# Small attentions of a two-layer kernel: keys masked once per group, scores contracted over 32 partitions

## The chip, the cores and the metric

The kernel runs on one core of a Trainium2 chip. The metric is the device time of one execution, in microseconds (us). Three runs of the kernel before gave a median of 2568.2 us (2562.18 to 2571.58). All data are float32 unless said otherwise.

## What is computed

The input x has 64 sequences of 64 rows with 128 features. Two layers run over it; the part that the change touches are two attentions with 16 heads of 8 features, in which every query row attends to 64 key rows:

```
# layer 0, feed-forward block: attention across the batch, for each of the 64 positions
q, k, v = split(LN(x) @ in_proj.T + in_proj_b)        # 16 heads of 8
a = softmax(q @ k.T / sqrt(8)) ; o = a @ v             # then out_proj, LN, mixture of experts
# layer 1: attention along the sequence, for each of the 64 sequences, causal
q, k, v = split(LN(x) @ w_qkv)                         # 16 heads of 8
a = softmax(mask(q @ k.T) / sqrt(128)) ; o = a @ v     # then out_proj
```

Around them stand a gated delta rule, two cross attentions with 16 heads of 32 features (layer 0), two mixtures of experts with routing, and a block with eight weighted projections (layer 1).

## The kernel before, in words

The 64 sequences are worked on in 16 groups (G) of four blocks of 64 rows, and four slots (s = 0 to 3) hold four groups at a time, with two PSUM banks each. The program of a group is written for each engine as a Python generator, and `in_order` interleaves the four slots' generators by a table of digits, `ORDER`, one table per phase and engine: each digit says which slot gives the next step. Each engine executes its queue in just that order, and semaphores tie the engines together. The phases are:

1. "one": delta rule and both cross attentions (`pe_delta`, `pe_mha` and so on).
2. "across": the attention across the batch (`pe_across`, which calls `pe_small` with y = "c", not causal).
3. "last": routing and experts of layer 0 (`pe_tiles`), then per group the causal attention (`pe_attn1`, which calls `pe_small` with y = "n", causal), the weighted projections (`pe_xattn1`, lines 1476 and 1482), and routing and experts of layer 1.

A small attention of one group has 16 heads, taken as four quads g = 0 to 3. Features lie on partitions: head h has partitions 8h to 8h + 7, so quad g has partitions 32g to 32g + 31. For each quad POOL builds masked keys (`pool_km`, line 994): km holds, for each block b and each of the quad's four heads j, the 64 keys with all partitions but head j's set to zero by a 0/1 mask (`m8`). PE then multiplies (`pe_scores`, lines 1001 and 1002): the block's 64 queries, all 128 partitions of them, are the stationary operand, and the 4 x 64 masked keys the moving one, so that one matmul gives four heads' scores of a block, written to the lower or the upper 64 partitions of PSUM as b is even or odd. In the causal attention a bfloat16 matmul with a constant of 128 partitions (`CB`, line 1001) first writes the causal mask, and the scores are added to it. Then follow the row maximum and the subtraction on DVE (1007, 1009), the exponential on ACT (1371), four transposes on PE (1013), a copy on ACT (1374) and the products with V on PE (1022), which also write to 64 partitions each. km has one buffer per slot: POOL makes the masked keys of quad g + 1 when the scores of quad g are done (signal `a_s`), and PE waits for `m_km` before each quad.

The cross attentions of phase "one" use the same `pool_km` and `pe_scores` with heads of 32 features and their own mask `m32`.

A matmul's record in the profile names rows and columns: 128*64 is a stationary operand of 128 partitions (the contraction) and 64 columns (the output partitions); below, such a pair is called the matmul's tile. A float32 matmul leaves two records, a bfloat16 one leaves one.

Of the kernel before, what the change touches and what calls it, by code (L numbers as in the profile page):

```python
# [18 lines left out]
W = 128 * NT  # L19
# [13 lines left out]
def columns(parts):  # L33
    at, out = 0, {}
    for name, n in parts:
# [7 lines left out]
    ("laterT", 64), ("causal", 64), ("m32", 4), ("parity", 2), ("m8", 16), ("m24", 4), ("tri", 64), ("half", 1), ("before", 128), ("ones", 128), ("iota", 128), ("part", 1), ("back", 8),  # L43
# [53 lines left out]
            "vz.c m_km.c.0 m_km.c.1 m_km.c.2 m_km.c.3",  # L97
# [45 lines left out]
            "rstd.n vz.n m_km.n.0 m_km.n.1 m_km.n.2 m_km.n.3 n_bias.n rstd.h rstd.g",  # L143
# [21 lines left out]
            "110332200001311330303222200102100001111000133010022122013302020112031020201012312110301000122131212120332023102120021020030301130323200222030310313001"  # L165
            "303110201201121031221320302133202102011213221123123021022132013212302021031300210212102230300300333013002301231330201301013221313120102312232110130332"
            "122000021211212210213001313202032321313331311232331112322311133000033122230313023220030032021131100330100103330122022130323020112313110201221120012213"
            "302331221323121023232021330131113302023023003022030300303032030012012010302011323330120211012001221231113122032021301123100132203321001201023032001201"
            "303123113230200220301330130102313132301201131010031223110100321222103211210022121213132031022233123233231211323233111230020201311022230331210322030302"
            "303200303001131103301010222021333021213132312112230130200011221123133321231230210232023210013013001132033023022303001203130130030113023102011210312321"  # L170
            "333021021120100212121122122131310230122021323102132102303303002302330320123200103031002303110323103230112210321322021321033112012200212113200013221302"
            "101021233002312133313112323312311223111300300222330031320322030012032003030303022022333011112021010231332121132131010212200012122313321233121232012303"
            "103232003203310010301113030022303030300032302002032323033120210221002113231311212033013203123310032112201003012032303112032103020133013001321302303102"
            "1213201130323230120102213030211232210213311231223123231121312322133131231232133132131323232123213131312313",
        "act":
            "110223300001311330033002332203002120102211210113311022130220132031020012000001132110203110211100220003222220300131130031212021331122333000022121132312"
            "210302201332001012102122003033000301332001213032011123210211312023033102211210002221110230012303200203310313113323211122300133113003131222301312122110"
            "323202133122012203332021332303031330020001333213231321102320211011132200222300033000323120012130313313220000112122313103210220311300022100030323101011"
# [30 lines left out]
        "dve":  # L209
            "20330112202303201320130123001220033221023311321103120310231002233020120332110131023102100231022032102311323101313201302132130213",  # L210
        "pool":
            "013202320230321103012203311010223032312103100231321102032023013102031221033110202213130103213213",
    },
    "last": {
        "pe":
# [285 lines left out]
def build(nc, x, ctx, ctxk, itok, cst, col, row, wa, ws, wf, wx, wl, x1, ys, out):  # L501
    es = ExitStack()
    with es:
# [80 lines left out]
        sig = Signals(nc)  # L584
# [1696 lines left out]
```

## Time and profile before

| | us |
|---|---|
| median of 3 runs | 2568.2 |
| profiled execution, whole | 2576.1 |
| profiled execution, span of the core | 2574.3 |
| PE busy in the span | 2194.3 (85%) |
| DVE busy | 1830.5 (71%) |
| POOL busy | 1469.8 (57%) |
| ACT busy | 1145.6 (45%) |
| masked keys on POOL (line 994), 256 instructions | 486.7 |
| scores on PE (line 1002), 2048 records | 291.7 |

Busy time is the union of an engine's instructions. Lines are those of the kernel before; PEld is the loading of stationary operands, which lies beside PE. Phase "one" ends at about 1345 us of the span, "across" at 1505 us, and the causal attention has its first mask matmul at 1812.0 us and its last at 2275.1 us.

### The profile page before, as it was taken

The numbers are of one execution on the slowest core, as the hardware profiler recorded it, in microseconds if no ns is written. First come the engines' busy times: TensorE is split into PE (matmuls) and PEld (weight loads), VectorE is DVE, ScalarE is ACT, GpSimd is POOL, SyncE is SP. The second block draws the span as 40 slices with busy tenths as digits, with TensorE's granted clock in tenths as the row PEclk, the third lists the DMA queues.
The fourth block names the chain that finished last, engine by engine and source line by source line (L and its number), as shares of the span: only waits on it lengthen the run. The fifth ranks groups of instructions, "written<-read, shape, count | busy, mean of one in ns | idle before, by whom it ended". The sixth has DMA issues, their size and how long they took to land.

```text
span 2574.3 us, 62932 instructions
## 1 busy us (share of the span) xinstructions
PE 2194.3 (85%) x24908; PEld 1758.7 (68%) x24908; DVE 1830.5 (71%) x4790; ACT 1145.6 (45%) x2561; POOL 1469.8 (57%) x1568
## 2 busy tenths in 40 slices
PE   5988989899898998889989963897798998996972
PEld 3866668666677666776667752887576776786972
DVE  6688777888778878688757788333788788875232
ACT  5234574356743466534545520453343343443541
POOL 3775447665567654676557864357746433413465
PEclk8999999899999999999999965898898998997996
DMA  3000000000000000000000002797000000006992
GB/s 128 4 5 1 1 1 4 4 2 1 2 4 4 2 1 2 3 5 2 1 34 2 2 18 98 240 361 219 22 20 11 18 16 3 14 19 218 346 331 81
DMA packets 85589, 144.99 MB, mean 56 GB/s; under 512 B 23664, under 2 KB 60016, under 8 KB 85040
## 3 DMA queue, kind: packets, MB, share of 16 engines
q1 hardware_dynamic: 76208, 122.33, 14.0%
q0 software_dynamic: 9088, 18.63, 2.7%
q8 instruction: 199, 3.26, 0.5%
q14 instruction: 94, 0.77, 0.1%
HBM read 124.40 MB, written 16.52 MB: 55 GB/s over the span
## 4 chain that ended last, share of the span: by engine, by line
PE 54%; DVE 25%; POOL 9%; issue 7%; DMA 3%; ACT 2%; SPq 0%; POOLq 0%; DVEq 0%; ACTq 0%
PE PS L1002 7%; PE PS L637 5%; PE PS L1022 5%; PE PS L1013 4%; PE PS L1482 3%; PE PS L1476 3%; PE PS L1946 3%; PE PS L1930 3%; POOL GOT L1633 3%; PE PS L627 2%; PE PS L989 2%; DVE z L618 2%; PE PS L1097 2%; PE PS L1086 1%; PE PS L1103 1%
## 5 line engine op out<-in xcount | busy, mean ns | idle before, releaser
L994 POOL TENSOR_TENSOR km<-qk,Cs 128x1024 f32<-128x1024 f32 x256 | 486.7, 1910 | 290.2 <-ACT qk L1141 149.3
L1002 PE MATMUL PS<-km,qk 128*64 128x256 f32 x2048 | 291.7, 395 | 0.2 <-POOL km L994 0.2
L1959 ACT ACTIVATE wh<-PS,we 128x128 f32<-128x128 f32 x624 | 175.5, 373 | 231.4 <-PE PS L1930 231.2
L1866 POOL DMA_INDIRECT wx<-x,INV x156 | 149.0, 955 | 159.4 <-PE PS L1937 83.9
L1007 DVE TENSOR_REDUCE mx<-PS 128x8 f32<-128x512 f32 x256 | 176.0, 688 | 81.3 <-PE PS L1002 79.3
L1022 PEld LDWEIGHTS PS<-V,PT 128*64 128x64 f32 x4096 | 155.4, 140 | 68.0 <-issue 32.4
L1946 PE MATMUL PS<-we,wh 128*128 128x128 f32 x1248 | 176.6, 287 | 21.1 <-DVE wxT L1976 19.1
L1022 PE MATMUL PS<-V,PT 128*64 128x66 f32 (+1 forms) x4096 | 179.6, 224 | 13.7 <-DVE PT L1179 9.1
L1009 DVE TENSOR_TENSOR P<-PS,mx 128x512 f32<-128x512 f32 x256 | 177.0, 691 | 8.8
L1946 PEld LDWEIGHTS PS<-we,wh 128*128 128x128 f32 x1248 | 160.9, 200 | 27.9 <-DVE wxT L1976 25.2
L1013 PE MATMUL PS<-Cs,P 128*128 128x128 f32 x1024 | 163.2, 286 | 16.1 <-ACT P L1371 8.4
L1930 PE MATMUL PS<-wxT,we 128*128 128x128 f32 x1248 | 171.8, 285 | 5.5 <-issue 3.0
L1002 PEld LDWEIGHTS PS<-km,qk 128*64 128x64 f32 x2048 | 147.4, 140 | 40.7 <-issue 15.8
L622 POOL TENSOR_TENSOR xrs<-xrs,Cs 128x2 f32<-128x2 f32 x112 | 82.0, 732 | 146.8 <-DVE xrs L614 144.3
L1497 ACT ACTIVATE eh<-PS 128x256 f32<-128x256 f32 x256 | 96.9, 383 | 154.3 <-PE PS L1476 151.0
L1930 PEld LDWEIGHTS PS<-wxT,we 128*128 128x128 f32 x1248 | 159.6, 201 | 7.9 <-issue 4.8
L1013 PEld LDWEIGHTS PS<-Cs,P 128*128 128x128 f32 x1024 | 116.6, 144 | 55.7 <-issue 21.9
L1633 POOL DMA_INDIRECT GOT<-ys,POS x128 | 123.6, 965 | 51.7 <-issue 49.7
L1476 PE MATMUL PS<-exF,WX 128*128 128x256 f32 x512 | 150.3, 399 | 3.1 <-DVE X L1526 2.9
L1482 PE MATMUL PS<-WX,eh 128*128 128x128 f32 x1024 | 138.1, 281 | 0.5 <-ACT eh L1497 0.5
L1482 PEld LDWEIGHTS PS<-WX,eh 128*128 128x128 f32 x1024 | 132.4, 196 | 8.0 <-issue 2.3
L1141 ACT ACTIVATE qk<-PS 128x512 f32<-128x512 f32 x128 | 76.4, 597 | 118.6 <-PE PS L1071 93.0
(337 smaller groups left out, 5344.0 us busy)
## 6 DMA issues: line engine op xcount, KB each, us to landing
we<-in_wf SPq DMA_DIRECT2D x78, 578.0 KB, 6.7
we<-in_wl SPq DMA_DIRECT2D x78, 578.0 KB, 6.6
ys<-wy SPq DMA_DIRECT2D x156, 64.0 KB, 6.2
x<-X SPq DMA_DIRECT2D x32, 128.0 KB, 2.0
R<-in_wa SPq DMA_DIRECT2D x1, 3072.0 KB, 15.5
wx<-x,INV POOLq DMA_INDIRECT x156, 5.6
X<-in_x SPq DMA_DIRECT2D x4, 512.0 KB, 15.3
WX<-in_wx SPq DMA_DIRECT2D x1, 2048.0 KB, 7.7
```

The costliest lines, as they stand in the source:

```text
L994: return e.tensor_tensor(A.km.rearrange("p (b j t) -> p b j t", b=NB, j=4), bc(v3(A.qk[:, W:2 * W], NB), 2, 4), bc(bc(masks, 1, NB), 3, 64 ...
L1002: i = e.matmul(o, A.qk[:, 64 * b:64 * b + 64], A.km[:, W * b:W * b + W], not causal, True)
L1007: e.tensor_reduce(A.mx, S3, AX, ALU.max).then_inc(*o.inc())
L1009: return e.tensor_tensor(v3(A.P, NA), S3, bc(A.mx, 2, 64), ALU.subtract)
L1013: i = e.transpose(dst[:, 128 * k:128 * k + 128], A.P[:, 128 * k:128 * k + 128], ID)
L1022: i = e.matmul(dst[64 * (b % 2):64 * (b % 2) + 64, c0:c0 + 2 * D + 2], A.PT[:, q0:q0 + 64], A.V[:, 8 * b + 2 * g + k, :, :].rearrange("p h ...
L1476: e.matmul(o, w1[:, x_, 128 * f:128 * f + 128], B.xF, True, True).then_inc(*sig.inc(G, "h_up", x_, f))
L1482: i = e.matmul(o[:, 128 * t:128 * t + 128], h[:, W * f + 128 * t:W * f + 128 * t + 128], w2[:, x_, f, :], f == 0, f == 1)
L1633: e.indirect_dma_start(out=GOT[G % 2][:, t, k, :], out_offset=None, in_=ys[h], in_offset=bass.IndirectOffsetOnAxis(ap=POS[h][:, j:j + 1], ...
L1930: i = e.matmul(ps(s, 1)[:, 128 * f:128 * f + 128], w[:, 128 * f:128 * f + 128], B.xT, True, True)
L1946: i = e.matmul(ps(s, 0)[:, 0:128], B.h[:, 128 * f:128 * f + 128], w[:, 644 + 128 * f:772 + 128 * f], f == 0, f == 3)
L1959: i = e.activation(B.h[:, 128 * f:128 * f + 128], ps(s, 1)[:, 128 * f:128 * f + 128], ACT.Relu, bias=w[:, 512 + f:513 + f])
```

## The change

POOL masks the keys once per group instead of once per quad. The new mask has four columns: column j keeps the partitions of the j-th head of every quad at once, so km holds the masked keys of all four quads, each quad's in its own 32 partitions. `pe_scores` gets a slice of partitions k; in the small attentions quad g contracts over partitions 32g to 32g + 31 of qk and km alone. The mask matmul with `CB` is left as it is, with 128 partitions. PE waits for `m_km` once per group; POOL issues one instruction per group in place of four, and no longer waits for `a_s`. The cross attentions call `pe_scores` with its default, all 128 partitions. All the tables of `ORDER` are new.

```diff
-        def pe_scores(e, A, dst, causal=False):
+        def pe_scores(e, A, dst, causal=False, k=slice(0, 128)):
             for b in range(NB):
                 r = slice(64 * (b % 2), 64 * (b % 2) + 64)
                 o = dst[r, W * (b // 2):W * (b // 2) + W]
                 if causal:
                     e.matmul(o, CB[:, r], bc(CB[:, 128:192], 1, 4), True, False)
-                i = e.matmul(o, A.qk[:, 64 * b:64 * b + 64], A.km[:, W * b:W * b + W], not causal, True)
+                i = e.matmul(o, A.qk[k, 64 * b:64 * b + 64], A.km[k, W * b:W * b + W], not causal, True)
             return i
...
             for g in range(4):
-                e.wait_ge(*sig.at(G, "m_km", y, g))
+                if g == 0:
+                    e.wait_ge(*sig.at(G, "m_km", y))
                 e.wait_ge(*(sig.at(G, "a_pt", y, g - 1) if g else sig.at(G, "n_v", y)))
                 if causal:
                     e.wait_ge(*cb.now())
-                pe_scores(e, A, ps(s, 1), causal).then_inc(*sig.inc(G, "a_s", y, g))
+                pe_scores(e, A, ps(s, 1), causal, slice(32 * g, 32 * g + 32)).then_inc(*sig.inc(G, "a_s", y, g))
...
-            for g in range(4):
-                e.wait_ge(*(sig.at(G, "a_s", y, g - 1) if g else sig.at(G, "m_qk", y)))
-                pool_km(e, A, c("m8", 4 * g, 4 * g + 4)).then_inc(*sig.inc(G, "m_km", y, g))
-                yield
+            e.wait_ge(*sig.at(G, "m_qk", y))
+            pool_km(e, A, c("m8")).then_inc(*sig.inc(G, "m_km", y))
+            yield
...
-    parts["m8"] = (r // 8) == np.arange(16)[None, :]
+    parts["m8"] = (r // 8) % 4 == np.arange(4)[None, :]
```

What the tables and the quads make of the queues is seen at three places. The first is POOL in phase "across", some way into it; km_296, km_311, km_326 and km_341 are the masked keys of slots 0 to 3, V the values' buffers. Before:

```order
L982 MEMSET V_309 128x576
L984 COPY V_309<-Cs 128x64
L994 TENSOR_TENSOR km_311<-qk_310,Cs 128x1024
L994 TENSOR_TENSOR km_296<-qk_295,Cs 128x1024
L994 TENSOR_TENSOR km_341<-qk_340,Cs 128x1024
L994 TENSOR_TENSOR km_296<-qk_295,Cs 128x1024
```

After:

```order
L982 MEMSET V_309 128x576
L984 COPY V_309<-Cs 128x64
L995 TENSOR_TENSOR km_311<-qk_310,Cs 128x1024
L982 MEMSET V_294 128x576
L984 COPY V_294<-Cs 128x64
L995 TENSOR_TENSOR km_296<-qk_295,Cs 128x1024
```

POOL now has one masking per group between the clearings of two V buffers, where it had four.

The second place is PE in phase "across" (1002 scores, 1013 transposes, 1022 products with V; in the changed kernel each line is one higher). Before:

```order
L1022 MATMUL PS<-V_339,PT_347 64x18 x8
L1002 MATMUL PS<-km_341,qk_340 64x256 x4
L1013 MATMUL PS<-Cs,P_298 128x128 x4
L1022 MATMUL PS<-V_324,PT_332 64x18 x8
L1013 MATMUL PS<-Cs,P_313 128x128 x4
L1022 MATMUL PS<-V_294,PT_302 64x18 x8
L1002 MATMUL PS<-km_296,qk_295 64x256 x4
L1022 MATMUL PS<-V_309,PT_317 64x18 x8
L1002 MATMUL PS<-km_311,qk_310 64x256 x4
```

After:

```order
L1023 MATMUL PS<-V_339,PT_347 64x18 x8
L1023 MATMUL PS<-V_294,PT_302 64x18 x8
L1014 MATMUL PS<-Cs,P_328 128x128 x4
L1003 MATMUL PS<-km_296,qk_295 64x256 x4
L1003 MATMUL PS<-km_341,qk_340 64x256 x4
L1023 MATMUL PS<-V_324,PT_332 64x18 x8
L1014 MATMUL PS<-Cs,P_313 128x128 x4
L1003 MATMUL PS<-km_326,qk_325 64x256 x4
```

The same kinds of work alternate in another order of slots. Over the whole phase a row of one tile is followed by a row of another 134 times before (128*64 and 128*128 alone), and 209 times after, with the scores as 32*64.

The third place is PE at one quad's scores in the causal attention. Before:

```order
L1022 MATMUL PS<-V_294,PT_302 64x18 x8
L1001 MATMUL PS<-CB 64x256
L1002 MATMUL PS<-km_296,qk_295 64x256
L1001 MATMUL PS<-CB 64x256
L1002 MATMUL PS<-km_296,qk_295 64x256
```

After:

```order
L1998 MATMUL PS<-Wsm,noF_338 128x128 x2
L1002 MATMUL PS<-CB 64x256
L1003 MATMUL PS<-km_296,qk_295 64x256
L1002 MATMUL PS<-CB 64x256
L1003 MATMUL PS<-km_296,qk_295 64x256
```

The alternation of mask and scores, four times per quad, is unmoved; but the mask keeps its 128 partitions while the scores have 32.

## Rows read from the trace of the kernel before

**Rows 1.** The page: busy time, share and instructions of each engine.

```profile
span 2574.3 us, 62932 instructions
...
PE 2194.3 (85%) x24908; PEld 1758.7 (68%) x24908; DVE 1830.5 (71%) x4790; ACT 1145.6 (45%) x2561; POOL 1469.8 (57%) x1568
```

**Rows 2.** Stretches of the span: length, busy time by engine, granted clock, DMA.

```profile
core 0: us, PE busy (x) PEld busy (x) DVE busy (x) ACT busy (x) POOL busy (x), PEclk, DMA share, GB/s
0.00:1345.00 1345.00, 1197.80 (x15744) 910.78 (x15744) 1056.13 (x2413) 673.16 (x1285) 801.19 (x910) 0.96 0.03 10
1345.00:1505.00 160.00, 156.40 (x2064) 115.28 (x2064) 116.79 (x279) 91.80 (x169) 126.03 (x90) 0.99 0.01 2
1505.00:1812.00 307.00, 212.62 (x1586) 198.26 (x1586) 165.35 (x617) 95.99 (x334) 181.51 (x217) 0.79 0.60 199
1812.00:2280.00 468.00, 418.70 (x3851) 335.71 (x3852) 382.41 (x1100) 180.69 (x419) 222.23 (x206) 0.93 0.05 13
```

**Rows 3.** Groups of instructions: busy us, mean ns; idle before them and its enders.

```profile
L994 POOL TENSOR_TENSOR km<-qk,Cs 128x1024 f32<-128x1024 f32 x256 | 486.7, 1910 | 290.2 <-ACT qk L1141 149.3 <-PE PS L1002 110.0 <-ACT qk L1364 26.7
L1001 PE MATMUL PS<-CB 128*64 128x256 bf16 x256 | 39.9, 290 | 7.7 <-POOL km L994 4.7 <-issue 2.8
```

**Rows 4.** The chain of waits by line, 1345 to 1505 us, then 1812 to 2280 us.

```profile
by line: PE PS L1002 35.0%; PE PS L1022 20.7%; PE PS L1013 20.3%; PE PS L1335 4.5%; PE PS L989 4.4%; PE PS L1336 3.2%; PE PS L627 3.2%; ACT PT L1374 1.9%; ACT P L1371 1.2%; DVE mx L1007 0.9%; DVE P L1009 0.9%; DVE est L607 0.9%; issue 0.9%;
...
by line: PE PS L1476 15.4%; PE PS L1482 14.7%; PE PS L1002 8.1%; PE PS L1022 5.7%; issue 5.1%; PE PS L1013 5.0%; POOL GOT L1633 4.9%; POOL km L994 3.2%; DVE epr L1510 2.7%; PE PS L627 2.7%; PE PS L1001 2.6%; DVE X L618 2.6%; DVE ez L618 2.1
```

**Rows 5.** Who waited for whom, 1812 to 2280 us: us in total, times, longest.

```profile
POOL km L994 <- PE PS L1002: 95.9, 35, 12.3
...
PE PS L1001 <- POOL km L994: 4.7, 3, 2.5
```

**Rows 6.** Timeline of PE at one causal quad: start us, us from first start to last end.

```profile
2061.09 0.31 PE L1001 MATMUL PS<-CB 128*64 128x256 bf16 x2
2061.22 0.60 PE L1002 MATMUL PS<-km,qk 128*64 128x256 f32 x4
2061.65 0.28 PE L1001 MATMUL PS<-CB 128*64 128x256 bf16 x2
2061.76 0.60 PE L1002 MATMUL PS<-km,qk 128*64 128x256 f32 x4
2062.30 0.48 PE L1476 MATMUL PS<-exF,WX 128*128 128x256 f32 x1
```

**Rows 7.** Timeline of PE in the first cross attention, all tiles 128*128 until line 1002.

```profile
179.78 0.60 PE L1070 MATMUL PS<-zx,R 128*128 128x256 f32 x2
180.21 0.59 PE L1071 MATMUL PS<-zy,R 128*128 128x256 f32 x2
180.74 0.65 PE L1002 MATMUL PS<-km,qk 128*64 128x256 f32 x4
```

**Rows 8.** Timeline of PE in the second cross attention, with a tile of 64 rows.

```profile
889.48 0.60 PE L1070 MATMUL PS<-zx,R 128*128 128x256 f32 x2
890.01 0.70 PE L1071 MATMUL PS<-zy,R 64*128 64x256 f32 x2
890.63 0.94 PE L1086 MATMUL PS<-R,oF 128*128 128x128 f32 x6
```

**Rows 9.** Timeline of PE in phase "across".

```profile
1403.40 0.66 PE L1013 MATMUL PS<-Cs,P 128*128 128x128 f32 x4
1403.98 0.67 PE L1022 MATMUL PS<-V,PT 128*64 128x18 f32 x16
1404.47 1.08 PE L1002 MATMUL PS<-km,qk 128*64 128x256 f32 x8
1405.36 0.30 PE L1022 MATMUL PS<-V,PT 128*64 128x18 f32 x5
```

**Rows 10.** Granted clock and the same columns, the first 60 us.

```profile
core 0: us, PE busy (x), PEclk, DMA share, GB/s
20.00:40.00 20.00, 10.21 (x25) 0.70 0.23 65
40.00:60.00 20.00, 14.45 (x125) 0.70 0.01 1
60.00:80.00 20.00, 19.49 (x450) 1.00 0.01 3
```

More of the change, by code:

```diff
@@ L42 @@
     ("ident", 128), ("sl", 128), ("unit", 64), ("le", 64), ("nm0", 64), ("nm1", 64), ("nm2", 64), ("nm3", 64), ("nm4", 64), ("nn", 64),
-    ("laterT", 64), ("causal", 64), ("m32", 4), ("parity", 2), ("m8", 16), ("m24", 4), ("tri", 64), ("half", 1), ("before", 128), ("ones", 128), ("iota", 128), ("part", 1), ("back", 8),
+    ("laterT", 64), ("causal", 64), ("m32", 4), ("parity", 2), ("m8", 4), ("m24", 4), ("tri", 64), ("half", 1), ("before", 128), ("ones", 128), ("iota", 128), ("part", 1), ("back", 8),
 ])
@@ L96 @@
         "pool":
-            "vz.c m_km.c.0 m_km.c.1 m_km.c.2 m_km.c.3",
+            "vz.c m_km.c",
     },
@@ L142 @@
         "pool":
-            "rstd.n vz.n m_km.n.0 m_km.n.1 m_km.n.2 m_km.n.3 n_bias.n rstd.h rstd.g",
+            "rstd.n vz.n m_km.n n_bias.n rstd.h rstd.g",
     },
@@ L168 @@
[L168 to L171, printed above, removed]
@@ new lines @@
+        "pool":
+            "013210122330110022033100020030011100011100112222220000221122011002302001311332022302133311111332122033221203133321233003133302000311230011131022103112"
+            "222013000320032303302113001213110311223022000002200112203330310033332210110100112133111003121020022220121113223230012333211113310233222103312221232331"
+            "230033333231021000313110120312103101332200001311133322200213010213123230011202231022333000002200223301011111330011222110033001123221222111022000022011"
+            "221113013333032122233102133022332212333320012133303303002111301230130130221331002002223333002100111233110021130230222211330003300221002200331033122111"
+            "102101113000312132202220212000110223331221110133110233322213013221233022123333002332333110300201131102301310322101332222333320000111213321323222023333"
+            "23",
@@ L252 @@
         "sp":
[L253 to L255 removed]
+            "576a1348db02c9dddddddddddd1133dddd22001504150246260437041537263726150415372604263175150437260426371504371265043715260437152604371526043715260437152630"
@@ L256 @@
+            "471526043715260347152604371564756745ab98dddda9b8ab9dddd8bdddda93382211dddd0037263726043715372615043701542615042637150426153702463175042615370426153704"
+            "2615042637153720641504263715372604cc01452637153726c04c04152637152307c46c46575c764ccccccccc",
     },
```

137 lines of the change are left out of this document (66 added, 71 removed).

## The prediction

> **What bounds the kernel now.** I read the page first: PE is busy 85% of the span, DVE 71%, POOL 57% [rows 1]. Since these are averages over unlike phases, I then cut the span at the phase borders [rows 2]. In "across" PE is busy 156.4 of 160.0 us, POOL 126.0; in the causal attention's stretch, 1812 to 2280 us, PE is busy 418.7 of 468 us, POOL 222.2. So both phases that the change touches run at PE's pace, and POOL, which the change relieves, has room. The chain of waits says the same: in "across" all its large items are PE's, and POOL's masking (line 994) isn't among the thirteen printed; in the causal stretch the masking has 3.2% of the chain [rows 4]. The waits show the direction [rows 5]: POOL waited 95.9 us for PE's scores, PE's mask matmul 4.7 us for POOL. POOL is held up by PE, hardly the other way round.
>
> **POOL's part.** The mask is made once per group: 32 maskings in place of 128 in the two small attentions. 96 go, at 1.91 us each [rows 3]: 183 us of POOL's busy time. In "across" I cost this at nothing: PE's 156.4 busy us cover it, and they stay. In the causal stretch the gain is at most the chain's 3.2% of 468 us, 15 us, at least PE's 4.7 us of waits; what then comes next in the chain is the same PE queue, so I take 8. The longer buffer life (km is now kept for four quads) delays POOL's next masking of the slot until the next group, three or more softmax rounds away; no wait on PE's side hangs on it.
>
> **PE's part: what one quad costs now.** A causal quad is four mask matmuls and four score matmuls, alternating. In the timeline they leave 2 + 4 + 2 + 4 records, and from the first start to the next line's start they take 2062.30 - 2061.09 = 1.21 us [rows 6]. The first four score records, two matmuls, pass in 2061.65 - 2061.22 = 0.43 us. One matmul of the same 256 columns with a tile of 128*128 also takes 0.43 us (180.21 - 179.78) [rows 7]. [...] The masks likewise: two in 0.13 us, and 0.11 us (2061.76 - 2061.65) for the second two.
>
> **What a change of tile costs.** In the first cross attention line 1071 follows 1070 with the same tile after 0.43 us; line 1002, with another, starts 0.53 us after 1071 [rows 7]: 0.10 us more. In the second cross attention 1071 has 64 rows: it starts 0.53 us after 1070, and the next line, again 128*128, 0.62 us after it [rows 8]. So a change in the number of **rows** alone costs 0.10 us on the way in, and the 0.19 us too many behind it are 0.10 us on the way out and 0.09 us more for the first matmul behind the change. [...] With 64 columns in place of 128 I take half of the 0.09, so **0.15 us per change**, between 0.10 and 0.19.
>
> [...]
>
> **PE's part: a causal quad afterwards.** The mask keeps 128 rows and the scores get 32, so every step of the alternation changes the tile. That costs twice. First, 7 changes inside a quad and one behind it. Second, the pairs are lost: the scores of block 0 must be through before the mask of block 1 may start, so nothing is left to run beside them. A quad becomes 4 masks at 0.11, 4 scores at 0.43, 7 changes at 0.15 and the leaving 0.10: 0.44 + 1.72 + 1.05 + 0.10 = 3.31 us, 2.10 more than the 1.21. There are 64 quads (256 mask records, four per quad [rows 3]): 134 us. With 0.10 per change it is 2.96 us, and 112 us in all; with 0.19, 3.59 us and 152 us. The stretch has 49 us in which PE is idle, a tenth of it; I let a tenth of the addition disappear there: **+121 us**.
>
> **PE's part: "across".** Here there is no mask matmul. A quad's scores stay together in one tile and keep their pairs: eight records took 0.89 us (1405.36 - 1404.47) between products with V, without a change [rows 9]. Only neighbours matter: in the program's order tile changes go from 134 to 209. 75 more at 0.15 us: **+11 us**, on a PE that is never idle; at 0.10 and 0.19 it is 8 and 14. [...]
>
> [...]
>
> **Phase "one"** (1345 us) does the same work in a new order. Nothing in it has a new cost; two orders of the same work can differ, for which I allow 10 us to both sides and take 0.
>
> **Sum**, against the profiled execution: 2576.1 + 121 - 8 + 11 = 2700 us. That execution is 7.9 us above the median of the three runs, so against the median: **2692 us**. This case's own range is 2692 with its terms at their ends: low, 112 us at four fifths, -15, +8, -10, which is +73 us, 2641; high, 152 - 5 + 14 + 10 = +171, 2739.
>
> **Rival 1: no change of tile (faster).** The 32-row matmuls may be run as 128*64 tiles whose other rows are empty, or the step from 128 to 32 rows may cost nothing. Then PE's times stay, the pairs too, and what is left is POOL's relief, up to 15 us, less some 20 changes of tile more by the new order in "across" (3 us): 2568 - 15 + 3 = 2556 us. It decides if a causal quad stays near 1.2 us. Against it stands the 64-row tile of [rows 8], which does pay. 10%.
>
> **Rival 2: changes cost, pairs stay.** If PE kept two blocks going side by side across the changes, a quad would get only 7 x 0.15 = 1.05 us more, 67 us in all, 60 behind the idle tenth: 2568 + 60 - 8 + 11 = 2631 us. Against it: the pairs exist only between neighbours in the queue of one tile. 8%.
>
> **Rival 3: the clock falls too.** [...] In the causal stretch it is 0.93, with PE busy 89%. Where PE was busy 69% it was 0.79 [rows 2], and in the first 60 us, with PE busy a half to three quarters, 0.70, and 1.00 only when it was busy throughout [rows 10]. The new quads stream nothing in 1.15 of their 3.31 us. That is 74 us of a stretch of then some 580. If this took the clock to 0.79, the stretch would grow by up to 0.93 / 0.79 = 1.18, some 100 us: 2790 us. Against it: PE is still working on something nearly always. 7%.
>
> **How the numbers follow.** The forecast (quads of 3.3 us) has 73%, rivals 10, 8 and 7%, and 2% are for POOL's relief or a better order making up for all of it. About 0.5%, 13 us, is what a measurement of this kernel can tell from no change. Slower: 73 + 8 + 7 = 88%. Rival 1 with its 12 us of gain lies at the bound, so its 10% and the 2% go 7 to faster and 5 to the same. The range holds the forecast's own and rival 2's value and ends below rival 3's, leaving out rivals 1 and 3 and the rest, 19%: 2625 to 2760 us.
>
> **What would show it.** Right: the timeline of a causal quad shows single mask records between score records, 0.8 us per block and 3.2 to 3.4 us per quad; mean durations of the score records rise; PE's busy time grows by 100 us or more while POOL's falls by 183; "across" is some 10 us longer in spite of an idle POOL; phase "one" is as long as before. Wrong: quads of 1.2 us (rival 1), of 2.2 us (rival 2), or a clock well under 0.9 in the causal stretch (rival 3). If "across" gets shorter, POOL did hold it up, and the reading of the first paragraph was at fault.

## The result, and the profile after: 278 us longer, most of it the clock

| | before | after |
|---|---|---|
| median, us (4 runs each) | 2568.55 | 2846.35 |
| lowest to highest, us | 2562.18 to 2571.58 | 2832.0 to 2854.08 |
| ratio (95% interval) | | 1.1072 (1.104 to 1.1104) |
| span of the profiled execution, us | 2574.3 | 2852.3 |

The changed kernel is 10.7% slower. The direction was forecast; the size, 2692 us with a range to 2760, was not. Line numbers of the changed kernel from 995 on are one higher than before: 1002 is the mask matmul, 1003 the scores, 1014 the transposes, 1023 the products with V, 1477 and 1483 the weighted projections, 995 POOL's masking.

First the page of the changed kernel: its span and its line of busy times, and the granted clock in the 40 slices (tenths of full speed).

```profile
span 2852.3 us, 62766 instructions
...
PE 2533.7 (89%) x24908; PEld 1900.9 (67%) x24908; DVE 1792.7 (63%) x4790; ACT 1138.2 (40%) x2554; POOL 1287.2 (45%) x1472
...
PEclk8999999999999999998555559975878688777996
```

Against [rows 1], PE is busy 339 us longer with the same 24908 records, and POOL 182.6 us shorter with 96 instructions fewer. So POOL's relief is there as forecast, and PE got slower. The clock line tells where. A slice is 71.3 us; a five is half of full speed. Fives stand from 1355 to 1711 us, that is in "across" and in the routing behind it, which had a low clock before too (0.79), and fives to eights in the causal attention from 1892 us on.

For a comparison stage by stage both spans are cut at the same places in PE's queue: shortly before the first and behind the last score matmul of "across", and at the first and last mask matmul of the causal attention. These are the stretches of the kernel before at these borders:

```profile
core 0: us, PE busy (x) PEld busy (x) DVE busy (x) ACT busy (x) POOL busy (x), PEclk, DMA share, GB/s
0.00:1333.00 1333.00, 1186.90 (x15648) 903.59 (x15648) 1050.78 (x2386) 668.54 (x1276) 792.19 (x901) 0.97 0.03 9
1333.00:1502.00 169.00, 164.43 (x2146) 119.88 (x2147) 119.35 (x290) 96.42 (x177) 133.15 (x96) 0.98 0.04 14
...
1812.00:2275.00 463.00, 413.70 (x3818) 331.54 (x3820) 377.87 (x1087) 177.54 (x411) 222.23 (x206) 0.93 0.05 14
```

And these are those of the changed kernel, with two short windows of "across" behind them:

```profile
core 0: us, PE busy (x) PEld busy (x) DVE busy (x) ACT busy (x) POOL busy (x), PEclk, DMA share, GB/s
0.00:1316.00 1316.00, 1185.41 (x15649) 899.59 (x15650) 1045.22 (x2386) 657.59 (x1269) 791.99 (x903) 0.97 0.03 9
1316.00:1587.00 271.00, 268.38 (x2146) 175.34 (x2147) 120.72 (x290) 96.62 (x177) 42.96 (x47) 0.58 0.03 9
1587.00:1892.00 305.00, 215.92 (x1607) 199.41 (x1606) 168.13 (x638) 97.05 (x336) 185.88 (x224) 0.79 0.60 200
1892.00:2555.00 663.00, 649.60 (x3815) 423.69 (x3815) 347.87 (x1084) 178.64 (x408) 127.57 (x154) 0.76 0.04 9
2555.00:2852.00 297.00, 214.38 (x1696) 202.92 (x1696) 110.72 (x393) 108.32 (x365) 138.83 (x147) 0.86 0.64 215
...
1330.00:1388.00 58.00, 58.00 (x438) 37.72 (x437) 21.77 (x41) 18.84 (x34) 3.60 (x5) 0.51 0.00 1
1389.00:1398.00 9.00, 9.00 (x98) 5.69 (x96) 7.12 (x24) 4.46 (x9) 6.63 (x7) 1.00 0.01 3
```

| stage | before, us @ clock | after, us @ clock | difference |
|---|---|---|---|
| phase "one" | 1333 @ 0.97 | 1316 @ 0.97 | -17 |
| "across" | 169 @ 0.98 | 271 @ 0.58 | +102 |
| routing and experts, layer 0 | 310 @ 0.79 | 305 @ 0.79 | -5 |
| causal attention and projections | 463 @ 0.93 | 663 @ 0.76 | +200 |
| the rest | 299 @ 0.86 | 297 @ 0.86 | -2 |

Both phases with small attentions got longer, and in both the clock fell. The two short windows are the most telling: for 58 us in "across" PE is not idle for a moment, and its clock is 0.51, about half of full speed; then, as busy as before, it has 1.00 for 9 us. The clock came back three times inside this phase, at some 1388, 1463 and 1522 us. Each time PE was at the projections of the next four groups (lines 1336, 1337 and 989, matmuls over 128 rows), which stand close together in the queue at 1380 to 1395, 1449 to 1466 and 1518 to 1530 us; between these places it was 0.50 (1399 to 1463 us, 1471 to 1521 and 1536 to 1587).

The chain of waits agrees. In "across" the scores have about the share of before, 36.8% for 35.0% [rows 4], because PE's groups got slower alike, as the timelines below show:

```profile
by line: PE PS L1003 36.8%; PE PS L1014 22.0%; PE PS L1023 22.0%; PE PS L1336 5.0%; PE PS L989 4.7%; PE PS L1337 3.6%; PE PS L627 3.0%; DVE P L1010 0.8%; DVE mx L1008 0.7%; ACT P L1373 0.5%; ACT CF L1424 0.2%; issue 0.2%; DVE est L607 0.2%;
```

The timeline of PE has both clocks. This is a part of a causal quad with the clock at 1.00 (2065 to 2068 us), and then of one at 0.50 (2100 to 2103 us):

```profile
2065.98 0.30 PE L1002 MATMUL PS<-CB 128*64 128x256 bf16 x1
2066.20 0.64 PE L1003 MATMUL PS<-km,qk 32*64 32x256 f32 x2
2066.78 0.30 PE L1002 MATMUL PS<-CB 128*64 128x256 bf16 x1
2067.00 0.64 PE L1003 MATMUL PS<-km,qk 32*64 32x256 f32 x2
...
2100.96 1.11 PE L1003 MATMUL PS<-km,qk 32*64 32x256 f32 x2
2102.00 0.42 PE L1002 MATMUL PS<-CB 128*64 128x256 bf16 x1
2102.35 1.11 PE L1003 MATMUL PS<-km,qk 32*64 32x256 f32 x2
```

At full clock it is what was forecast: mask and score alternate one by one, where before they went in pairs, and a block takes 2066.78 - 2065.98 = 0.80 us. A pair are the matmuls of two blocks, b even and b odd, that pass in the time of one: in the timeline of before, 2061.2 to 2061.3 us, two score records lie within 0.39 us, while the mean of one is 379 ns (1002 in that quad), and all four records of the two matmuls pass in 0.43 us [rows 6]. At half clock a block takes 2102.35 - 2100.96 = 1.39 us. The phase "across" at half clock (0.50 from 1436 to 1448 us), to be laid beside [rows 9]:

```profile
1441.84 1.12 PE L1014 MATMUL PS<-Cs,P 128*128 128x128 f32 x4
1442.89 1.07 PE L1023 MATMUL PS<-V,PT 128*64 128x18 f32 x16
1443.89 1.97 PE L1003 MATMUL PS<-km,qk 32*64 32x256 f32 x8
```

Transposes and products, which the change doesn't touch, have gone from 0.66 and 0.67 us to 1.12 and 1.07, eight score records from 1.08 to 1.97.

So two questions are open. **What takes the clock down**: the stalls at the tile changes (that was rival 3), or the 32 rows themselves? "Across" has few changes of tile and was at half clock for most of its time (0.58 in the mean), which speaks against the stalls. And how much is left when the clock is taken out? The runs that follow were to tell these apart.

### The profile page after: what moved, and what is told of

It is laid out like the page before. It is cut to its first block, busy times and chain, and to the rows that moved or that the text cites. A ratio compares the mean times of both kernels' runs of the same rounds, so it can differ in the third digit from the quotient of the medians.

```text
span 2852.3 us, 62766 instructions
## 1 busy us (share of the span) xinstructions
PE 2533.7 (89%) x24908; PEld 1900.9 (67%) x24908; DVE 1792.7 (63%) x4790; ACT 1138.2 (40%) x2554; POOL 1287.2 (45%) x1472
## 4 chain that ended last, share of the span: by engine, by line
PE 65%; DVE 17%; POOL 7%; issue 6%; ACT 2%; DMA 2%; SPq 0%; POOLq 0%; DVEq 0%; ACTq 0%
PE PS L1003 14%; PE PS L1023 6%; PE PS L1014 5%; PE PS L637 5%; PE PS L1483 4%; PE PS L1477 4%; PE PS L1947 3%; PE PS L1931 3%; PE PS L627 3%; PE PS L1002 2%; PE PS L989 2%; DVE z L618 2%; POOL GOT L1634 1%; DVE cv L827 1%; POOL wx L1867 1%
## 5 line engine op out<-in xcount | busy, mean ns | idle before, releaser
L1003 PE MATMUL PS<-km,qk 128*64 128x256 f32 (+1 forms) x2048 | 462.2, 466 | 0.5 <-POOL km L995 0.5
L995 POOL TENSOR_TENSOR km<-qk,Cs 128x1024 f32<-128x1024 f32 x160 | 303.8, 1903 | 249.9 <-ACT qk L1142 153.5
L1003 PEld LDWEIGHTS PS<-km,qk 128*64 128x64 f32 (+1 forms) x2048 | 173.9, 157 | 98.4 <-issue 61.9
L1023 PEld LDWEIGHTS PS<-V,PT 128*64 128x64 f32 x4096 | 182.8, 165 | 81.0 <-issue 54.9
L1023 PE MATMUL PS<-V,PT 128*64 128x66 f32 (+1 forms) x4096 | 210.2, 243 | 8.6 <-ACT PT L1133 4.0
L622 POOL TENSOR_TENSOR ers<-ers,Cs 128x2 f32<-128x2 f32 x64 | 45.5, 712 | 377.6 <-DVE ers L614 376.3
L1014 PE MATMUL PS<-Cs,P 128*128 128x128 f32 x1024 | 202.8, 338 | 9.7 <-ACT P L1129 8.1
L1014 PEld LDWEIGHTS PS<-Cs,P 128*128 128x128 f32 x1024 | 146.6, 172 | 60.5 <-issue 39.4
L1376 ACT ACTIVATE PT<-PS 128x512 f32<-128x512 f32 x128 | 76.3, 596 | 219.7 <-PE PS L1014 218.9
L1483 PEld LDWEIGHTS PS<-WX,eh 128*128 128x128 f32 x1024 | 147.3, 214 | 8.9 <-issue 3.2
```

The source lines that it names most:

```text
L995: return e.tensor_tensor(A.km.rearrange("p (b j t) -> p b j t", b=NB, j=4), bc(v3(A.qk[:, W:2 * W], NB), 2, 4), bc(bc(masks, 1, NB), 3, 64 ...
L1003: i = e.matmul(o, A.qk[k, 64 * b:64 * b + 64], A.km[k, W * b:W * b + W], not causal, True)
L1014: i = e.transpose(dst[:, 128 * k:128 * k + 128], A.P[:, 128 * k:128 * k + 128], ID)
L1023: i = e.matmul(dst[64 * (b % 2):64 * (b % 2) + 64, c0:c0 + 2 * D + 2], A.PT[:, q0:q0 + 64], A.V[:, 8 * b + 2 * g + k, :, :].rearrange("p h ...
L1483: i = e.matmul(o[:, 128 * t:128 * t + 128], h[:, W * f + 128 * t:W * f + 128 * t + 128], w2[:, x_, f, :], f == 0, f == 1)
```

## Experiments on the clock and the tile changes

The runs with 128 rows, with 64 rows, with the masks first and with the order of before ran on a chip on which the kernel before took 2646.07 us (median of 7), so their totals are compared as ratios. The difference lies in the phases of routing and experts (338 us there for 305 to 310 in layer 0); phase "one" takes 1316 us on either chip with the new order, and "across" 168 us with 128 rows. The stretches are therefore set beside each other directly.

**All 128 rows again.** Everything of the change but its slice.

```diff
-                pe_scores(e, A, ps(s, 1), causal, slice(32 * g, 32 * g + 32)).then_inc(*sig.inc(G, "a_s", y, g))
+                pe_scores(e, A, ps(s, 1), causal).then_inc(*sig.inc(G, "a_s", y, g))
```

Each score is then a sum over a head of every quad, which is another computation; the work's shape and timing are those of 128 rows.

> The changed kernel with its queues and its one masking per group, but with all 128 partitions in the scores of the small attentions (so quad g's scores are summed over the four quads, another result than the reference's). Theory A (the 32 rows are the cause, by changes of tile and by the clock): everything is undone but POOL's relief and the new order, 2550 to 2570 us, phase across 155 to 165 us at a clock of 0.95 or more, causal quads of 1.2 us. Theory B (the new order of the queues costs a good part): well above 2600 us.

Measured: 2593.77 us against 2646.07, ratio 0.9813 (0.9788 to 0.9838). The two stretches:

```profile
1316.00:1484.00 168.00, 165.29 (x2145) 120.22 (x2145) 119.32 (x289) 97.16 (x177) 43.19 (x48) 0.99 0.04 14
...
1822.00:2244.00 422.00, 394.25 (x3806) 324.57 (x3804) 346.42 (x1085) 176.52 (x408) 127.94 (x154) 0.97 0.06 15
```

Without the slice the change gains 1.9%. All of its loss is in the slice, and what is left of it gains more than the 8 us of the forecast: the causal stretch is 422 us where it was 463, with a clock of 0.97 for 0.93.

**64 rows.** The tile still changes at each step between mask and scores, as with 32.

```diff
-                pe_scores(e, A, ps(s, 1), causal, slice(32 * g, 32 * g + 32)).then_inc(*sig.inc(G, "a_s", y, g))
+                pe_scores(e, A, ps(s, 1), causal, slice(64 * (g // 2), 64 * (g // 2) + 64)).then_inc(*sig.inc(G, "a_s", y, g))
```

A score is then the sum over a head of each of two quads.

> The changed kernel with the 64 partitions that hold the quad (two quads' scores are summed, another result than the reference's): as many changes of tile as with 32. Theory A1 (the clock falls because of the stalls at changes of tile): the same as with 32 rows, 2830 to 2860 us, phase across about 255 us. Theory A2 (the clock falls with the number of rows in use, even where PE is busy): clearly less, 2690 to 2780 us, phase across 170 to 210 us with a clock of 0.75 to 0.95, while the causal quads at full clock still take 3.2 us.

Measured: 2730.18 us, ratio 1.0336 (1.0294 to 1.0378). Two stretches, and between them the same 58 us that were at half clock in the changed kernel:

```profile
1317.00:1490.00 173.00, 170.56 (x2148) 117.22 (x2147) 120.04 (x290) 98.16 (x177) 42.68 (x46) 0.99 0.04 13
...
1330.00:1388.00 58.00, 57.96 (x738) 39.30 (x735) 40.01 (x88) 32.57 (x58) 10.99 (x12) 1.00 0.01 2
...
1835.00:2372.00 537.00, 520.08 (x3817) 352.26 (x3816) 348.93 (x1085) 176.51 (x408) 127.98 (x154) 0.98 0.04 12
```

And a piece of a causal quad:

```profile
2101.05 0.30 PE L1002 MATMUL PS<-CB 128*64 128x256 bf16 x1
2101.28 0.64 PE L1003 MATMUL PS<-km,qk 64*64 64x256 f32 x2
2101.85 0.30 PE L1002 MATMUL PS<-CB 128*64 128x256 bf16 x1
2102.07 0.64 PE L1003 MATMUL PS<-km,qk 64*64 64x256 f32 x2
```

The quad is the same as with 32 rows at full clock, 0.80 us per block. Four blocks make 3.2 us. The stalls are all there, and the clock stays at 0.98. In the window of 58 us PE got 738 records done instead of 438, with the same queue and the same busy share. So the stalls don't take the clock. Nor is it the partial fall of theory A2: with 64 rows none of the clock is lost, and the ratio stands for some 2655 us on the chip of the result, below A2's range. This run also has the forecast's own terms with nothing else in them: the tile changes and the lost pairs are 537 - 422 = 115 us in the causal stretch, and 173 - 168 = 5 us in "across".

**33 rows.** With 32 rows the clock fell and with 64 it didn't. One row more than 32 can behave as the one or as the other; the profile names the tile of this run 33*64.

```diff
-                pe_scores(e, A, ps(s, 1), causal, slice(32 * g, 32 * g + 32)).then_inc(*sig.inc(G, "a_s", y, g))
+                pe_scores(e, A, ps(s, 1), causal, slice(64 * (g // 2), 64 * (g // 2) + 33)).then_inc(*sig.inc(G, "a_s", y, g))
```

The scores are again not those of the heads alone.

> The changed kernel with 33 partitions in the scores, 0 to 32 or 64 to 96 (another result than the reference's), which is one more row than 32. If the clock follows the number of rows in use: phase across 240 us or more at 0.5 to 0.7, 1.08 or more in all. If it follows the tile (a 32-row tile against a 64-row one): as the 64-row run, phase across 170 to 178 us at 0.97 or more, 1.025 to 1.045 in all.

Measured: 2841.15 us against 2567.99, ratio 1.1052 (1.1007 to 1.1097).

```profile
1316.00:1582.00 266.00, 264.97 (x2144) 172.30 (x2144) 120.32 (x288) 96.57 (x177) 42.94 (x47) 0.59 0.03 9
...
1888.00:2537.00 649.00, 634.21 (x3814) 413.65 (x3813) 348.54 (x1085) 178.25 (x408) 128.00 (x154) 0.78 0.04 10
```

The clock of 33 rows, 0.59 and 0.78, is that of 32 (0.58 and 0.76), not that of 64 (0.99 and 0.98). How it goes between 33 and 64 rows no run shows.

**Masks first.** The 32 rows stay, but nearly all changes of tile inside a quad go: the causal mask is written by two matmuls of 512 columns ahead of the four score matmuls.

```diff
+            for b in range(2 if causal else 0):
+                r = slice(64 * b, 64 * b + 64)
+                e.matmul(dst[r, 0:2 * W], CB[:, r], bc(CB[:, 128:192], 1, 8), True, False)
...
-                if causal:
-                    e.matmul(o, CB[:, r], bc(CB[:, 128:192], 1, 4), True, False)
-                i = e.matmul(o, A.qk[k, 64 * b:64 * b + 64], A.km[k, W * b:W * b + W], not causal, True)
+                i = e.matmul(o, A.qk[k, 64 * b:64 * b + 64], A.km[k, W * b:W * b + W], not causal, not causal or b >= 2)
```

> The changed kernel, with the causal mask written by two matmuls of 512 columns ahead of a quad's four score matmuls in place of four of 256 between them: two changes of tile per quad in place of eight, and the pairs of blocks are back. Theory A1 (the clock follows the stalls): the causal stretch is back to 480 to 500 us at 0.9 or more, phase across stays at 255 us, 2650 us in all. Theory A2 (the clock follows the rows): the stalls go, 64 times about 1.7 us, but the clock in the causal stretch stays near 0.75, 2700 to 2740 us in all.

Measured: 2712.57 us, ratio 1.0267 (1.0234 to 1.03).

```profile
1316.00:1572.00 256.00, 252.87 (x2145) 165.46 (x2143) 120.31 (x289) 96.48 (x177) 42.66 (x46) 0.62 0.02 9
...
1909.00:2345.00 436.00, 414.77 (x3680) 323.04 (x3682) 346.22 (x1085) 176.20 (x408) 127.48 (x154) 0.94 0.06 14
```

By its clocks, and by its ratio, which stands for some 2637 us on the chip of the result, this run alone would fit theory A1; the run with 64 rows is what rules A1 out. The causal stretch is back at 436 us: 14 more than with 128 rows, at 0.94. "Across", which has no mask, stays at 0.62. So the stalls alone don't take the clock (64 rows), but the loss isn't set by the row count alone either: with the same 32-row scores in shorter quads, the causal stretch keeps its clock. In "across" the small attentions are nearly all of PE's work; in the causal stretch they share it with the projections, and the less time the 32-row quads fill, the less clock is lost. That last sentence is a reading, which no run measured apart. What fits it is that in the changed kernel's "across" the clock came back among the projections alone, and that it did so in this run, with rises at some 1384, 1446 and 1508 us.

**The order of before.** The changed kernel with `ORDER` as it was, and three empty steps in POOL's generator so that the table fits.

```diff
             pool_km(e, A, c("m8")).then_inc(*sig.inc(G, "m_km", y))
             yield
+            for g in range(1, 4):
+                yield
```

> The changed kernel, 32 rows and one masking per group, with the queues in the order of the kernel before. Theory A (the order matters little): within 15 us of the changed kernel, 2830 to 2860 us. Theory B (the new order costs): 2780 us or less.

Measured: 2897.64 us, ratio 1.0975 (1.0926 to 1.1024).

```profile
0.00:1330.00 1330.00, 1185.38 (x15649) 903.12 (x15649) 1047.16 (x2386) 668.46 (x1276) 794.06 (x902) 0.97 0.03 9
1330.00:1567.00 237.00, 232.21 (x2145) 154.85 (x2146) 120.28 (x290) 96.83 (x177) 43.41 (x47) 0.68 0.03 10
...
1902.00:2529.00 627.00, 612.43 (x3821) 405.59 (x3820) 352.88 (x1088) 177.81 (x411) 130.45 (x158) 0.82 0.04 10
```

The new order isn't the cause; with the old one the clock falls too, though less: 0.68 for 0.58 in "across" and 0.82 for 0.76 in the causal stretch, which are 34 and 36 us shorter than with the new order. So the order may set a part of the loss; but "across" took 256 us in the run with the masks first and 271 in the changed kernel, with the same queue, so a good part of such a difference needs no cause of this kind. Nor do all rises of the clock in "across" stand among the projections here: two of the four later ones lie elsewhere, at some 1494 and 1552 us. What the new order does bring is phase "one", 1316 us instead of 1330.

**The order of before, 128 rows.** Both of the above together: only POOL's masking is left of the change. The edit beside the last kernel:

```diff
-                pe_scores(e, A, ps(s, 1), causal, slice(32 * g, 32 * g + 32)).then_inc(*sig.inc(G, "a_s", y, g))
+                pe_scores(e, A, ps(s, 1), causal).then_inc(*sig.inc(G, "a_s", y, g))
```

> One masking per group, 128 rows in the scores (another result than the reference's), and the queues in the order of the kernel before. It parts POOL's relief from the new order in the 0.981 of the 128-row run. If the new order makes the gain: phase one 1330 us or more, causal stretch as before, 0.995 to 1.00. If POOL's relief makes it: only phase one is 17 us longer than with the new order, 0.985 to 0.99.

Measured: 2535.9 us against 2567.99, ratio 0.9865 (0.9842 to 0.9888); phase "one" 1331 us, "across" 168, the causal stretch 428. POOL's relief alone is worth 1.35%, or 32 us in the medians, in the old order and the old tiles. The forecast had 8, and 15 as its upper bound.

## Experiments on POOL's relief: its work or its waits

In the kernel before, POOL waited 95.9 us of the causal stretch for PE's scores [rows 5]. Two things went with the three maskings per group: those waits, behind which POOL's other work stood, and 1.9 us of work each. Two runs put back one each, on top of the last kernel.

**The waits alone.**

```diff
             for g in range(1, 4):
+                e.wait_ge(*sig.at(G, "a_s", y, g - 1))
                 yield
```

> As the run in the old order with 128 rows (0.9865), but POOL keeps its three later waits per group for PE's scores, with no work behind them (another result than the reference's). If the waits, which hold up all that is queued behind them on POOL, made the loss of the kernel before: 0.995 to 1.00. If the 1.9 us of work made it: 0.985 to 0.99.

Measured: 2537.14 us against 2569.2, ratio 0.9879 (0.9856 to 0.9902); causal stretch 428 us, as without the waits.

**The work alone.** Three further maskings of the same size per group, from a constant into a buffer that nobody reads; nobody waits for them, and they wait only for the one before.

```diff
             for g in range(1, 4):
+                if kd.n:
+                    e.wait_ge(*kd.now())
+                e.tensor_tensor(A.kd.rearrange("p (b j t) -> p b j t", b=NB, j=4), bc(v3(Cs[:, 0:W], NB), 2, 4), bc(bc(c("m8"), 1, NB), 3, 64), ALU.mult).then_inc(*kd.inc())
                 yield
```

> As the run in the old order with 128 rows (0.9865), but POOL makes three more maskings per group into a buffer that nobody reads, from a constant, waiting for nothing but its own last one (another result than the reference's). If POOL's work made the loss of the kernel before: 0.995 to 1.00, and phase across at 168 us. If the waits made it: 0.985 to 0.99.

Measured: 2589.18 us against 2569.2, ratio 1.0074 (1.0051 to 1.0097); causal stretch 479 us. Work for which nobody waits costs 2589.18 - 2535.9 = 53 us, more than the kernel before had lost by it, and 51 us lie in the causal stretch. "Across" has half of the extra maskings too, POOL busy 133.98 us there for 43.09, and it stays at 168 us. The groups of DVE in the causal stretch show how the time is lost. Without the extra work:

```profile
L1513 DVE SCALAR_TENSOR_TENSOR epr<-eit,ecx 128x128 f32<-128x128 int32 x112 | 38.8, 347 | 2.0
...
L618 DVE TENSOR_SCALAR ez<-X,emv,ers 128x128 f32<-128x128 f32 x30 | 14.4, 521 | 1.2 <-POOL ers L622 1.1
...
L1529 DVE SCALAR_TENSOR_TENSOR X<-PS,egt,X 128x128 f32<-128x128 f32 x208 | 62.6, 345 | 17.8 <-PE PS L1485 15.8 <-DVE X L1529 0.5
```

With it:

```profile
L1518 DVE SCALAR_TENSOR_TENSOR epr<-eit,ecx 128x128 f32<-128x128 int32 x112 | 53.2, 475 | 2.0
...
L620 DVE TENSOR_SCALAR ez<-X,emv,ers 128x128 f32<-128x128 f32 x30 | 22.9, 804 | 1.2 <-POOL ers L624 1.1
...
L1534 DVE SCALAR_TENSOR_TENSOR X<-PS,egt,X 128x128 f32<-128x128 f32 x208 | 62.5, 344 | 23.1 <-PE PS L1490 21.4 <-DVE X L1534 0.5
```

The first two groups have their operands in SBUF, and one instruction of them takes 475 ns for 347 in the mean, and 804 for 521. The medians don't move (292 ns for 291, and 342 for 341): most of them keep their length, and a few are held for up to some 2 us. The third group reads PSUM and SBUF and stays at 345. DVE is busy 351.20 us of the stretch in the one and 399.79 in the other, and five groups with operands in SBUF account for all of the 48.6 us between them: 14.4 and 8.5 in the two above, 8.8, 12.0 and 5.0 in three more. In "across", where DVE's large groups read PSUM, it is busy 119.19 us without the extra work and 119.15 with it.

There is another way in which such work could cost time, since POOL's later instructions stand behind it. It is small here: in the causal stretch PE's waits for DVE grow from 19.0 to 40.1 us and those for ACT from 4.2 to 12.0, but those for POOL only from 0 to 1.8, and all waits of other engines for POOL from 6.9 to 11.5. PE idles 60 us in place of 27, and its clock is 0.93 for 0.96.

In the kernel before it can be seen at a single pair, from the timelines of POOL and DVE:

```profile
2065.70 1.91 POOL L994 TENSOR_TENSOR km<-qk,Cs 128x1024 f32<-128x1024 f32 x1
...
2065.08 2.61 DVE L618 TENSOR_SCALAR ez<-X,emv,ers 128x128 f32<-128x128 f32 x2 [0.32 <-POOL ers L622]
2067.61 0.28 DVE L1510 SCALAR_TENSOR_TENSOR epr<-eit,ecx 128x128 f32<-128x128 int32 x1
```

The masking ends at 2065.70 + 1.91 = 2067.61 us, and in that moment DVE's next instruction starts, behind two that together took 2.61 us. So DVE is held while POOL masks. With the extra work `epr`, which has two SBUF inputs, takes 475 ns for 347 in the mean, and the group that takes one of its inputs from PSUM doesn't change (344 ns for 345). `ez` has one large SBUF input, beside two columns of scalars, and is held as well (804 ns for 521). Why they are held no run shows.

## Experiments on a better version

The scores can have 128 rows and one masking per group at once, if the queries are masked too: with all queries but quad g's set to zero, the other quads' keys in km add nothing.

**Masked queries on POOL.** One more POOL instruction per group, of the masking's size, makes four copies of the queries, each with one quad's 32 partitions; PE's scores take copy g (the lines for the buffer and for `pe_scores` are left out here).

```diff
-            pool_km(e, A, c("m8")).then_inc(*sig.inc(G, "m_km", y))
+            pool_km(e, A, c("m8"))
+            e.tensor_tensor(v3(A.qm, 4), bc(A.qk[:, 0:W], 1, 4), bc(c("m32"), 2, W), ALU.mult).then_inc(*sig.inc(G, "m_km", y))
```

> The changed kernel with one masking of the keys and one of the queries per group (four copies of the queries, each with one quad's partitions), and scores over all 128 partitions: POOL has 2 x 1.9 us per group of a small attention in place of 4 x 1.9 before and 1 x 1.9 in the changed kernel, PE no 32-row tile. Theory A2 (all the loss comes from the 32-row tile, by changes and by the clock): as the 128-row run, 0.98 to 0.99 of the kernel before. If POOL's one masking, and not two, was what gained there: 0.99 to 1.00.

Measured: 2546.43 us against 2567.99, ratio 0.9906 (0.9883 to 0.993). "Across" takes 186 us, with PE busy 168.91 of them; the causal stretch 436. The clock is 0.97 in both. "Across" is 18 us longer than with 128 rows alone (168), and PE is idle for 17 of its 186 us: 14.9 us of that are waits of the scores for the masked queries, which are POOL's second instruction in a row. This run says something on the clock too. Three quarters of each stationary operand are zeros, so that no more products differ from zero than with 32 rows, and the clock is 0.97 where 32 rows had 0.58 and 0.76. So in these runs it went with the rows that an instruction has, not with those that hold something.

**The same, and the causal masks in two matmuls of 512 columns.**

```diff
-                if causal:
-                    e.matmul(o, CB[:, r], bc(CB[:, 128:192], 1, 4), True, False)
+                if causal and b < 2:
+                    e.matmul(dst[r, 0:2 * W], CB[:, r], bc(CB[:, 128:192], 1, 8), True, False)
...
```

> As the run with masked queries, and the causal mask of a quad written by two matmuls of 512 columns in place of four of 256. As many columns are streamed, so theory: within 0.5% of it, at best 6 us faster by fewer instructions.

Measured: 2545.55 us, ratio 0.9908 (0.9887 to 0.993), the same as the last within its interval. With one tile throughout, fewer mask matmuls bring nothing.

**Masked queries on ACT.** ACT copies the queries from PSUM anyway, and is busy 45% of the kernel before and 47% of this one. It now writes them four times, with the mask as the scale of each activation, and the bias masked likewise; the keys are copied first and have a signal of their own, so that POOL can start.

```diff
-                e.activation(A.qk, ps(s, 0), ACT.Copy).then_inc(*sig.inc(G, "m_qk", y))
+                e.activation(A.qk[:, W:2 * W], ps(s, 0)[:, W:2 * W], ACT.Copy).then_inc(*sig.inc(G, "m_k", y))
+                for g in range(4):
+                    i = e.activation(A.qm[:, W * g:W * g + W], ps(s, 0)[:, 0:W], ACT.Copy, scale=c("m32", g, g + 1))
...
```

> One masking of the keys per group on POOL, and the four masked copies of the queries made by ACT straight from PSUM (four activations of 128x256 with the 0/1 mask as scale, about 0.4 us each, in place of one copy), beside POOL's masking; scores over all 128 partitions. Theory: PE and POOL as in the 128-row run, ACT has 32 x 1.3 = 42 us more, which 45% busy cover; the 18 us that phase across lost by the second masking on POOL are won back: 0.98 to 0.985 of the kernel before. If ACT's longer step holds the first quad up: as with queries masked on POOL, 0.99.

Measured: 2518.34 us (2517.39 to 2521.68) against 2569.2, ratio 0.9809 (0.9792 to 0.9827). Its two stretches:

```profile
1317.00:1497.00 180.00, 167.95 (x2145) 120.45 (x2146) 119.67 (x290) 118.78 (x226) 43.69 (x48) 0.98 0.04 13
...
1804.00:2221.00 417.00, 392.02 (x3813) 323.28 (x3810) 343.73 (x1081) 192.96 (x466) 127.97 (x154) 0.98 0.06 15
```

It computes what the reference asks and is faster than both kernels: 51 us below the kernel before, 328 below the changed one. "Across" is 11 us longer than before, with PE idle for 12 of its 180 us, most of it waiting for ACT; of the 18 us that it lost with the queries masked on POOL, 6 are won back. The causal stretch is 46 us shorter, phase "one" 16.

## Why the prediction was right or wrong

| step of the prediction | forecast, us | measured, us | from |
|---|---|---|---|
| changes of tile and lost pairs, causal | +121 | +115 | 537 - 422, 64 against 128 rows |
| changes of tile, "across" | +11 | +5 | 173 - 168, 64 against 128 rows |
| POOL's relief, causal | -8 | -35 | 428 - 463, old order and 128 rows |
| phase "one", new order | 0 | -17 | 1316 - 1333 |
| the clock, causal | 0 (rival 3) | +126 | 663 - 537, 32 against 64 rows |
| the clock, "across" | 0 | +98 | 271 - 173, 32 against 64 rows |

Added up these are +292 us; the spans differ by 278. The remaining 14 are steps that the table leaves out: 7 in routing, experts and the rest (-5 and -2), 6 in the causal stretch, which with 128 rows has 428 us in the old order and 422 in the new, and 1 in "across" (169 before, 168 with POOL's relief). Each size is that of one step behind the other; the two rows on the clock hold for the new order.

**What bounds the kernel.** That both phases run at PE's pace held. For the clock it was the worst case: in "across" PE was busy 268.38 of 271 us at a clock of 0.58, and hardly anything of what the clock cost could pass in idle time.

**The quad.** This was the best step. A change of tile, taken from a cross attention hundreds of microseconds away [rows 7, 8], and pairs that are lost gave 3.31 us for a quad. It takes 3.2, and the stretch grew by 115 us, 121 forecast. Rivals 1 and 2 (quads of 1.2 and 2.2 us) are out. The 0.15 us of one change were an estimate, made of the starts in [rows 7, 8], and no run shows that term by itself: the scores start 2066.20 - 2065.98 = 0.22 us behind the mask, the next mask 0.58 us behind the scores, which is 0.80 us a block where 0.11 + 0.43 + 2 x 0.15 = 0.84 was forecast. What the trace of before does show at a change is the loading: 1071's stationary operand is loaded from 180.00 us, 0.21 ahead of its matmul, where the tile stays, and from 890.01 us, together with it, where the tile has 64 rows, with PEld idle for 0.33 us before. In "across" PE's rows change tile 156 times with 128 rows in the new order and 209 times with 64 or 32, and the 53 changes cost 5 us, some 0.09 each in place of 0.15. The "tenth that disappears in idle time" was about right as well: 64 quads of 3.2 - 1.21 = 1.99 us are 127 us, and 115 showed.

**The clock: the step that failed.** The sum had no term for it, that is, it took the granted clock as unchanged; rival 3 did have one, with 7%, in the causal stretch alone, and with the stalls as its mechanism. The runs show three faults in this. The mechanism was another: 64 rows have the stalls of 32 and a clock of 0.98; 33 rows lose it like 32 (0.78 and 0.76 in the causal stretch). So the place was wrong too: "across", which has few stalls more, went to 0.58. And the size of 100 us was that of the lowest stretch seen before, 0.79, while the clock went to 0.76 and 0.58. Together the two stretches lost 224 us by it, more than by all other terms. "PE is still working on something nearly always" was the argument against rival 3, and it was true and beside the point: at 0.51 PE was busy 58.00 of 58.00 us.

Could the trace have told? It had no float32 matmul with 32 rows. The delta rule of phase "one" has tiles of 64*64, and the phase's clock was 0.97; that speaks for 64 rows and says nothing of 32. The highest clock in the trace of before is 1.00 [rows 10] and the lowest 0.50 (1505 to 1560 us, PE busy 19.92 of 55 us); for a row count that it doesn't show, the honest bounds were these two, in both phases where such matmuls are most of PE's work. Half clock on 160 and 468 us would have been an upper end of several hundred, and a chance well above 7%.

At full clock fewer rows didn't make a matmul shorter: the two records of one with 256 columns take 0.64 us with 32 and with 64 rows, behind a mask of 128 rows, and 0.60 with 128, behind the same tile [rows 7].

**POOL's relief.** Right in sign, four times too small. The bounds were made from POOL's own share of the chain and from those who waited for POOL. But POOL's work did most of its harm without a wait for POOL: it held some of DVE's instructions. That stood in the trace before, as an `ez` pair of 2.61 us; and `epr` and `ez` of DVE, 2.7% and 2.1% of the chain [rows 4], were read as DVE's own. Part of the 35 us is clock: the stretch had 0.93 before and 0.96 after the relief, with PE idle 49 and 27 us.

**Phase "one".** Two orders of the same work differ by 17 us (1330 to 1337 us in all runs with the old table, 1316 to 1318 in all with the new one), a little outside the 10 allowed. Which part of the order does it stays open.

## What to carry to other kernels

When a matmul is to contract over fewer partitions than any in the trace of before, that trace says nothing of its granted clock, and the range has to hold the clock as a term of its own, from the highest to the lowest that the trace shows (here 1.00 and 0.50). Here 58 us of "across", with PE never idle, had 0.51 with 32 rows and 1.00 with 64, and the whole kernel took 2846.35 us for 2568.55. A matmul of 32 rows saved nothing by itself (0.64 us for its two records, 0.60 with 128), and masking with zeros over 128 rows was the faster way to the same sum (2518.34 us for 2569.2). Look at where matmuls alternate between tiles: in the causal stretch the changes and the lost pairs cost 115 us (537 us with 64 rows, 422 with 128), and a quad took 3.2 us for 1.21. And cost an instruction of POOL not only by who waits for it, but by which instructions of DVE have run beside it and got longer (48 maskings for which nobody waited cost 51 us there).

## What the runs showed of the hardware that was not expected

- The granted clock was lower with 32 and 33 rows than with 64 and 128, at equal busy time: in the same 58 us of "across" PE was busy throughout and had 0.51 with 32 rows and 1.00 with 64. In the whole phase it was 0.58, 0.59, 0.99 and 0.99 with 32, 33, 64 and 128 rows, and 0.97 with 128 rows of which three quarters are zeros. Why, no run shows.
- The loss depends on the mixture too: in the changed kernel's "across" the three rises of the clock stood among projections over 128 rows (in the run with the old order two of four did), and the causal stretch had 0.76 with 32 rows in quads of 3.2 us at full clock and 0.94 with the same scores behind two mask matmuls.
- A masking of POOL of 1.9 us for which nobody waits is free or not by what DVE does beside it: 48 of them in the causal stretch cost 51 us, by way of DVE instructions with operands in SBUF (521 to 804 ns for one in the mean), and 48 in "across", where DVE reads PSUM, cost nothing.
- Matmuls that write the lower and the upper 64 partitions of PSUM run side by side (two in 0.43 us, the time of one with a tile of 128*128 [rows 6, 7]), and the records in the profile group them otherwise than the program does: 2 + 4 + 2 + 4 [rows 6] where the queue has mask and score one by one. With 32 or 64 rows in the scores and 128 in the masks the records alternate one by one, and the pairs are gone (0.80 us per block).
